# Third down piece made in the next expert's first tile, and the down-weight load placed behind the turned product

## The reference, cut to what matters

```
logits = x @ gate_weight.T ; topk_w, topk_idx = top_k(softmax(logits), 8) ; topk_w /= sum(topk_w)
for every expert e, over the tokens that picked it:
    g = tokens @ w_gate[e]          # 1024 -> 384
    u = tokens @ w_up[e]            # 1024 -> 384
    out = (silu(g) * u) @ w_down[e] # 384 -> 1024
y[token] = sum over its 8 experts of topk_w * out
```

## Time and profile before

| what | value |
| --- | --- |
| median of three runs | 6529.13 us (6527.38 to 6531.33) |
| the profiled execution, its own time | 6549.64 us |
| its span, first to last instruction | 6548.0 us |
| PE busy | 6384.2 us (97%) |
| PE weight loads busy | 5657.9 us (86%) |
| DVE, ACT, POOL busy | 3679.3 (56%), 2889.7 (44%), 2091.6 us (32%) |
| granted TensorE clock, mean over the span | 0.991 |

### The profile page before, as it was taken

How to read it: one execution, slowest core, us unless ns; L and a number is a source line. 1 busy time by engine, 2 the same in 40 slices (tenths; PEclk the granted TensorE clock), 3 DMA queues, 4 the chain that set the end, 5 groups by cost and what they waited for, 6 DMA issues and landing times.

```text
span 6548.0 us, 105789 instructions
## 1 busy us (share of the span) xinstructions
PE 6384.2 (97%) x31912; PEld 5657.9 (86%) x31913; DVE 3679.3 (56%) x4585; ACT 2889.7 (44%) x3319; POOL 2091.6 (32%) x1889
## 2 busy tenths in 40 slices
PE   9999998999999999889999999999999999999998
PEld 7888887887888788779989999999999999999997
DVE  4443434999999899845454455443533444444444
ACT  3222224888888755433343344332422333333333
POOL 1010000000000145644444454444444444444444
PEclk9999999999999999989999999999999999999999
DMA  8754565555555576557676676665755556666666
GB/s 279 244 193 147 148 148 145 130 128 126 126 130 130 144 202 173 134 134 191 164 219 167 175 200 175 170 161 112 194 112 110 139 140 170 147 159 168 164 156 157
DMA packets 844890, 1049.59 MB, mean 160 GB/s; under 512 B 440705, under 2 KB 638081, under 8 KB 844802
## 3 DMA queue, kind: packets, MB, share of 16 engines
q0 software_dynamic: 123984, 368.70, 25.1%
q1 hardware_dynamic: 564432, 382.50, 23.6%
q10 hardware_dynamic: 156386, 297.29, 13.3%
HBM read 725.85 MB, written 322.31 MB: 160 GB/s over the span
## 4 chain that ended last, share of the span: by engine, by line
PE 49%; DMA 2%; issue 2%; DVE 2%; another core or an unknown queue 1%; POOL 1%; ACT 1%; DVEq 1%; ACTq 0%; POOLq 0%; SPq 0%
PE moe_ps_gate L1400 6%; PE moe_ps_gate L1402 5%; PE moe_ps_gate L1401 5%; PE moe_ps_y L1389 5%; PE moe_ps_y L1388 5%; PE moe_ps_up L1401 5%; PE moe_ps_up L1400 5%; PE moe_ps_up L1402 5%; PE moe_ps_y L1387 5%; PE moe_ps_hT L1407 1%; DMA moe_tokens<-h2st,moe_rows 1%; DMA first_raw<-in_w_up 1%; POOL moe_tokens L1342 1%; DVE moe_gu_lo L1508 0%
## 5 line engine op out<-in xcount | busy, mean ns | idle before, releaser
L1342 POOL DMA_INDIRECT moe_tokens<-h2st,moe_rows x1156 | 1228.8, 1063 | 1942.7 <-DVE moe_rows L1518 1674.3
L1400 PE MATMUL moe_ps_gate<-moe_gu_hi,moe_xT_hi 128*128 128x384 f32 x2288 | 794.5, 347 | 61.5 <-DVE moe_xT_lo L1512 43.5
L1401 PE MATMUL moe_ps_gate<-moe_gu_lo,moe_xT_hi 128*128 128x384 f32 x2288 | 769.3, 336 | 0.0
L1400 PE MATMUL moe_ps_up<-moe_gu_hi,moe_xT_hi 128*128 128x384 f32 x2288 | 764.9, 334 | 4.2 <-DVE moe_gu_lo L1508 4.2
L1402 PE MATMUL moe_ps_gate<-moe_gu_hi,moe_xT_lo 128*128 128x384 f32 x2288 | 768.2, 336 | 0.0
L1402 PE MATMUL moe_ps_up<-moe_gu_hi,moe_xT_lo 128*128 128x384 f32 x2288 | 764.3, 334 | 0.0
L1401 PE MATMUL moe_ps_up<-moe_gu_lo,moe_xT_hi 128*128 128x384 f32 x2288 | 764.2, 334 | 0.0
L1531 DVE SCALAR_TENSOR_TENSOR moe_hidden<-moe_hidden,moe_rec_w,moe_ps_up 128x384 f32<-128x384 f32 x286 | 175.3, 613 | 989.1 <-PE moe_ps_up L1402 798.4
L1436 ACT CAST moe_xT_hi<-moe_ps_turned 128x1024 fp32r<-128x1024 f32 x287 | 291.3, 1015 | 908.0 <-PE moe_ps_up L1402 709.0
L1524 DVE STREAM_TRANSPOSE moe_ps_turned<-moe_tokens 128x1024 f32<-128x1024 f32 x288 | 362.5, 1259 | 569.9 <-DMA moe_tokens<-h2st,moe_rows 554.8
L1389 PE MATMUL moe_ps_y<-moe_d_hi,moe_hT_lo 128*128 128x512 f32 x1722 | 676.6, 393 | 0.0
(11 more groups left out here) (205 smaller groups left out, 13426.0 us busy)
## 6 DMA issues: line engine op xcount, KB each, us to landing
first_raw<-in_w_gate ACTq DMA_DIRECT2D x63, 1536.0 KB
first_raw<-in_w_up ACTq DMA_DIRECT2D x63, 1536.0 KB
moe_raw_d<-in_w_down ACTq DMA_DIRECT2D x63, 1536.0 KB
proj_a_raw<-in_ctxT POOLq DMA_DIRECT2D x64, 512.0 KB, 5.7
kst<-proj_o SPq DMA_DIRECT2D x256, 128.0 KB, 2.8
vst<-proj_o SPq DMA_DIRECT2D x64, 512.0 KB, 2.6
qst<-proj_o SPq DMA_DIRECT2D x256, 128.0 KB, 2.2
att_kt<-kst SPq DMA_DIRECT2D x64, 512.0 KB
```

Source lines behind the costliest of these rows:

```text
L1342: nc.gpsimd.indirect_dma_start(out=tokens[:, g * (H // G):(g + 1) * (H // G)], out_offset=None, in_=h2_quarters, in_offset=bass.IndirectOf ...
L1400: nc.tensor.matmul(o[:, 0:I], xT_hi[:, c], gu_hi[:, b, k, c], start=(c == 0), stop=False)
L1401: nc.tensor.matmul(o[:, 0:I], xT_hi[:, c], gu_lo[:, b, k, c], start=False, stop=False)
```

## The change

On DVE, `split` behind an expert's last tile ends one piece earlier, so it makes pieces 4 and 5 only. Piece 6, the third low piece of the down weights, is made in the new expert's own first tile, behind `hidden` and `tokens_low` and ahead of the gate and up pieces for the expert after. The same holds for the very first expert and for the last. ACT still makes the high parts of all seven pieces where it did. On ACT, `load_down` stands behind `turned_high` and no longer between pieces 0 and 1.

```
@@ ACT @@
                 def first_tile(t, e, b, more):
                     tokens_high(t + 1)
-                    split(e, b, 0, 1)
+                    split(e, b, 0, 2)
+                    turned_high(t)
                     load_down(e)
-                    split(e, b, 1, 2)
-                    turned_high(t)
                     split(e, b, 2, 3)
                     output(t - 1)
                     split(e, b, 3, GU)
@@ DVE @@
-                def tile(t, e=None, b=None):
+                def tile(t, e=None, b=None, own=None):
...
                     tokens_low(t + 1)
+                    if own is not None:
+                        split(own, 1 - b, PIECES - 1, PIECES)
                     if e is not None:
                         split(e, b, 0, 3)
                     turn_tokens(t + 2)
...
-                split(0, 0, GU // 2, PIECES)
+                split(0, 0, GU // 2, PIECES - 1)
...
                 def expert(e, b, has_next, has_second):
                     if has_next:
-                        expert_tiles(dve, e, lambda t: tile(t, e + 1, 1 - b), tile)
-                        split(e + 1, 1 - b, GU, PIECES)
+                        expert_tiles(dve, e, lambda t: tile(t, e + 1, 1 - b, e), tile)
+                        split(e + 1, 1 - b, GU, PIECES - 1)
                     else:
-                        expert_tiles(dve, e, tile, tile)
+                        expert_tiles(dve, e, lambda t: tile(t, None, 1 - b, e), tile)
```

## The result

| | kernel before | changed kernel |
| --- | --- | --- |
| median, same session | 6529.45 us (6527.38 to 6536.07, 6 runs) | 6555.22 us (6552.07 to 6560.64, 6 runs) |
| profiled execution, its span | 6549.64, 6548.0 us | 6560.64, 6559.0 us |
| PE busy, share of the span | 6384.2 us, 97% | 6389.3 us, 97% |

The ratio is 1.0039 (95% interval 1.0029 to 1.005). The change makes the kernel 25.8 us slower, clear of the 0.2% that a measurement can tell. The forecast was +9 us, the range up to +39.

The account below looks back on a forecast made before the run. PE, 97% busy, was taken as the bound, with some 50 us lost in the experts' pass. From the profiled 6549.6 us, +12.3 (branch) and -3.0 (load) gave 6558.9; the +9.3 carried to the median: 6538 us, range 6522 to 6568.

Parts of the forecast that it names:

- The likeliest case: Whole kernel: the forecast of 6538 us, given chance 0.50 with its own range of 6530 to 6546 us.
- the slower cases: Outcomes slower than the 0.2% band: forecast's upper part 0.10, unmoved header 0.18, long branch stall 0.08; together 0.36.
- Step 1: DVE, first tiles: without piece 6 ahead, `hidden` and the tokens' low part come 1.14 us earlier where DVE holds them.
- DVE's long header doesn't move: Rival, chance 0.18: in 25 first tiles `hidden` stays put and piece 6 adds some 1.1 us each; 6567 us.
- Steps 2 and 3: PE, first tiles' ends: wait renamed from tokens' low part to piece 6, sum 0.0 us; branch behind it adds 0.32 us.
- step 3: PE's wait now stands on the branch: 0.32 us more, 42 of 56 first tiles later, +12.3 us in sum.
- First ends: PE's loss from first tiles' down product to next tile, against 4.37 us, over 56 tiles: 11.4 us, forecast +12.3.
- The base: Profiled execution lies 20.5 us above the runs' median; the difference of +9.3 us was taken to carry over.
- Step 4: Six one-tile experts: PE waits for the next gate piece, 1.7 us behind piece 6, which hides the branch; 0 us.
- Step 5: DVE's later first-tile work starts at the old time or up to 0.2 us later, covered by over 1 us; 0 us.
- Step 6: `load_down` about 3 us later delays nothing and frees the token gather behind two-tile experts; about -3 us.

Follow-up runs that it names:

- e1: The kernel before run again with no edit, with a new profile: 6533.21 us, ratio 1.0002.
- e7: The changed kernel without PE's wait for all seven pieces, with pieces 5 and 6 both made behind the tokens' low part: 6561.11 us, ratio 1.0046.
- e5: The changed kernel with PE's wait for all seven pieces moved off the branch to the head of each further tile: 6551.64 us, ratio 1.0030.
- e4: The changed kernel with PE's wait for all seven pieces at a first tile's end left out: 6547.31 us, ratio 1.0022.
- e3: The changed kernel with `load_down` back between pieces 0 and 1, so only piece 6 is moved: 6559.46 us, ratio 1.0037.
- e2: The kernel before with only `load_down` moved behind `turned_high`, all pieces at their old places: 6546.6 us, ratio 1.0023.
- e6: The changed kernel without PE's wait for all seven pieces, two thirds of the down load at the old place, one third behind `turned_high`: 6546.6 us, ratio 1.0025.
- e11: The kernel before with `load_down` behind silu at the first tile's end, just ahead of the gate load: 6591.66 us, ratio 1.0057.
- e9: The kernel before with `load_down` behind `output` on ACT, pieces untouched: 6554.76 us, ratio 1.0032.
- e10: The kernel before with `load_down` between the gate and the up load, pieces untouched: 6621.48 us, ratio 1.0134.

## Why the prediction was right and where it was not

The range (6522 to 6568) held the time, and the sign was among the slower cases that I had given 0.36. The likeliest case missed by 17 us. By the prediction's own sign (a tile's average moves by more than 0.05 us) it was wrong: 22.8 us over 285 tiles are 0.08 us against e1; against the profile of before, 12.7 us, they are 0.045.

*Step 1, hidden 1.14 us earlier: in part.* In 20 of the 21 odd-numbered experts behind four or more tiles `hidden` moves from 2.25 (e1) to 0.80 on the scale, 1.45 us; in the 15 even-numbered ones from 2.52 to 1.83 as a rule, 0.69 us, and its "issue" grows from 1.52 to 1.94 us. One odd-numbered expert, DVE with PE's zero, in e1 and in the changed kernel:

```profile
4844.73 0.61 DVE L1531 SCALAR_TENSOR_TENSOR moe_hidden<-moe_hidden,moe_rec_w,moe_ps_up 128x384 f32<-128x384 f32 x1 [1.27 <-issue]
```
```profile
4842.46 0.39 PE L1387 MATMUL moe_ps_y<-moe_d_hi,moe_hT_hi 128*128 128x512 f32 x1
```
```profile
4853.64 0.61 DVE L1530 SCALAR_TENSOR_TENSOR moe_hidden<-moe_hidden,moe_rec_w,moe_ps_up 128x384 f32<-128x384 f32 x1 [0.98 <-PE moe_ps_up L1402]
```
```profile
4852.80 0.39 PE L1387 MATMUL moe_ps_y<-moe_d_hi,moe_hT_hi 128*128 128x512 f32 x1
```

So the rival "DVE's long header doesn't move" holds by half in every second expert, and these are the late ones: 13 of the 15 have a second tile, and in 12 of these piece 6 makes PE start at 5.16 to 5.39. What binds this header was not found; in e7, with one piece ahead of it, it costs nothing.

*Steps 2 and 3, the wait renamed, with the branch on top: right.* PE waits for the down piece 15 times (three of them behind one-tile experts). The distance is 0.48 us, where I had taken 0.32; e5 gives 0.24 of it to the branch. First ends go from 3.9 us (e1) to 16.5 us: +12.6, and the sum of step 3 said +12.3. That agreement is partly luck. I had the waits of the old profile (11.4 us) as the base and 0.32 us on 42 of 56 tiles; in truth the base is 3.9 us, and 15 tiles pay 0.79 us or more each. The sentence "Where DVE is the bound, five pieces of work in another order end at the same time" was right; but in the typical execution DVE is just not the bound there (tokens' low part at 4.27 in even experts, 0.05 us under the limit), so the third piece, which was behind nobody before, is now the last to come.

*The base: the failed step.* "The profiled execution is 20.5 us above the median of the runs; the difference of +9.3 us carries over." It does not. Ten of these 20 us lie in the pass that is changed (3698.3 against 3688.2 us), at the very places that the argument was about (first ends 11.4 against 3.9 us, ends behind one-tile experts 13.9 against 10.1). The "remote" waits ahead of them are absent in e1 and in the changed kernel. Against e1 the profiled difference is 6559.0 - 6535.3 = 23.7 us. Against the old profile it is 11.0 us, close to the forecast's 9.3, but by other terms: first ends +5.1 us and not +12.3, the down product's waits +7.6 us and not 0.

*Step 4, one-tile experts at 0 us: wrong, and by the prediction's own mechanism.* "The branch is hidden under this piece." It is not. Behind a one-tile expert PE passes the branch and the next expert's header, and in the changed kernel it starts 2.2 to 2.7 us behind the end of piece 6 (0.48 at the other first ends). The first gate piece is ready 1.7 to 1.9 us behind piece 6, so PE is late for it by a part: its distance from the gate piece is 0.49 to 0.88 us, six times, where in e1, e4 and e5 it is 0.05 or 0.06 us, six times each. The ends behind these six experts are 4.1 us longer than in e1, and e5 has 3.9 of it back, more than it gains at all first ends together (2.5 us). One such place in the changed kernel, then in e5, which has the wait off the branch. The first of the three pieces in the `x3` row takes 1.75 us and ends at 5784.16 and at 5777.94:

```profile
5781.28 1.21 DVE L1507 TENSOR_TENSOR moe_d_lo<-moe_raw_d,moe_d_hi 128x1024 fp32r<-128x1024 f32 x1
5782.41 5.09 DVE L1507 TENSOR_TENSOR moe_gu_lo<-first_raw,moe_gu_hi 128x1536 fp32r<-128x1536 f32 x3
5784.98 0.44 PE L1400 MATMUL moe_ps_gate<-moe_gu_hi,moe_xT_hi 128*128 128x384 f32 x1 [1.55 <-DVE moe_gu_lo L1507]
```
```profile
5776.19 5.09 DVE L1507 TENSOR_TENSOR moe_gu_lo<-first_raw,moe_gu_hi 128x1536 fp32r<-128x1536 f32 x3
5778.00 0.45 PE L1402 MATMUL moe_ps_gate<-moe_gu_hi,moe_xT_hi 128*128 128x384 f32 x1 [0.80 <-DVE moe_gu_lo L1507]
```

*Step 5, DVE's later work at 0 us: wrong in e7, open in the changed kernel.* PE's waits for the turned product's low part, 7.9 us in e1, are 11.7 us after the change and 29.2 in e7. In e7 they stand behind experts with two tiles too. In the changed kernel four of the five, 11.2 us, stand behind one-tile experts, where DVE itself waits for up weights (next).

*Step 6, the load later, -3 us: the wait goes as predicted, the gain does not come.* The turning of tokens behind two-tile experts waits no more, as predicted: 0 us in 11 places against 17.3 us (16.0 in e1). But the changed kernel is no faster than e3, which has the piece moved and the load in its old place. The answer to the earlier trace rows in the changed kernel, DVE, ACT and POOL:

```profile
4045.40 1.25 DVE L1523 STREAM_TRANSPOSE moe_ps_turned<-moe_tokens 128x1024 f32<-128x1024 f32 x1
```
```profile
4041.75 0.40 ACTq L1453 DMA_DIRECT2D moe_raw_d<-in_w_down  x1
```
```profile
4040.22 1.07 POOL L1342 DMA_INDIRECT moe_tokens<-h2st,moe_rows  x1 [0.30 <-issue]
```

Here the load is behind the last gather issue, and the load alone (e2) shows the other side. Behind a one-tile expert the gate, up and down weights queue back to back, and ACT waits there for the up weights, 3.37 us in e1 and 4.11 us after the change. The down load was issued at 5783.77 after the change and at 5765.70 in e1, 1.21 us ahead and 4.56 us ahead of the next expert's first matmul (5784.98 and 5770.26). Then (ACT in e1, ACT after, PE after):

```profile
5788.71 1.48 ACT L1430 CAST moe_gu_hi<-first_raw 128x1536 fp32r<-128x1536 f32 x1 [3.37 <-DMA first_raw<-in_w_up]
```
```profile
5805.75 1.48 ACT L1430 CAST moe_gu_hi<-first_raw 128x1536 fp32r<-128x1536 f32 x1 [4.11 <-DMA first_raw<-in_w_up]
```
```profile
5810.80 0.79 PE L1387 MATMUL moe_ps_y<-moe_d_hi,moe_hT_hi 128*128 128x512 f32 x1 [3.06 <-DVE moe_hT_lo L1540]
...
5814.32 0.39 PE L1389 MATMUL moe_ps_y<-moe_d_hi,moe_hT_lo 128*128 128x512 f32 x1
```

The up weights come 18.45 us behind that first matmul in e1 and 20.77 us after the change; PE's wait there is 0.56 us in e1 and 3.06 us now. It is tempting to blame the later down load. The record speaks against it: in e2 this load stands as late as in the changed kernel (4.95 us behind the down product's start in both), and the up weights still come 18.39 us behind that first matmul:

```profile
5793.65 1.48 ACT L1430 CAST moe_gu_hi<-first_raw 128x1536 fp32r<-128x1536 f32 x1 [3.38 <-DMA first_raw<-in_w_up]
```

With the piece moved they come at 20.80 us in e3, 20.03 in e4 and 21.22 in e5, and at 20.68 in the profiled run of e6, with two thirds of the load early. PE's waits for the turned product's low part behind the six one-tile experts say the same: 7.4 us in e1 and 4.6 in e2, but 8.7 in e3, 11.2 in the changed kernel, 12.5 in e5 and 15.5 in e4. The single places scatter (behind the first one-tile expert e1 has 22.01 us), and how moving the piece delays the up weights stays open.

*The account.* Against e1, the changed kernel's 22.8 us: first ends +12.6 (forecast +12.3); ends behind one-tile experts +4.1 (10.1 to 14.2; forecast 0); down product +3.8 (7.9 to 11.7; forecast 0); up pieces -2.8 (5.3 to 2.5); loop exits and ends of other tiles +1.2; the load's -3 of the forecast is not found. That is 18.9. The rest, 3.9 us, is of the size of what TensorE's clock costs (last section).

## What to carry to other kernels

A piece of work that is moved off one chain is put in front of another: before moving it, ask of each later item on that engine (here the turning of tokens and the low part of the turned product) how much room it has, and of each wait whose meaning changes without an edit what it now waits for and what stands behind it, on both sides of a branch. Take the base of a sum from more than one profile, and if the profiled execution is out of the range of the timed ones, find the waits that make it so before a difference is carried over. A load is early or late only against the other transfers: place it by what is issued next to it, and try the experts with the least work, where loads queue back to back.

## What the runs showed of the hardware

*TensorE's clock behind a wait.* In the experts' pass of the changed kernel there are seven stretches of 3.4 us at half clock (1.2 GHz), each beginning within 1.5 us of the end of an idle time of PE of 1.80 to 3.53 us. In the profile of before one of 2.11 us is followed by none. Stretches of the changed kernel, with busy times and counts, then granted clock, DMA share and GB/s:

```profile
3328.70:3332.30 3.60, 0.13 (x1) 0.00 (x0) 3.48 (x5) 2.76 (x4) 0.00 (x0) 1.00 1.00 376
3332.40:3335.80 3.40, 3.40 (x9) 2.68 (x10) 2.10 (x3) 1.01 (x1) 2.76 (x2) 0.55 0.78 220
3336.00:3339.40 3.40, 3.40 (x19) 2.92 (x18) 1.01 (x1) 0.70 (x2) 2.49 (x4) 0.97 1.02 357
```

PE was idle for 3.53 us ahead of 3332.36. At 5810.80, above, the same happens behind 3.06 us: eight matmuls take until 5814.32, 3.52 us, where eight take 1.95 us in e1 at the same tile. So this wait cost 1.6 us more than its own length. Within the pass the half clock covers 10.2 us in e1 (three stretches) and 23.9 us after the change (seven). At 1.6 us each the four more are an estimate of some 6 us, somewhat more than the rest of the account.

*One kernel, two levels.* The medians of the kernel before were 6529 to 6533 us in five sets of runs and 6552.36 us (9 runs) in the sixth, on a chip that served no other experiment. The profiled time of before, 6549.64 us, lies within the sixth set (6545.23 to 6555.07) and above all runs of the others (at most 6539.05). There e11's silus show the "remote" wait (14 of them), as in the profile of before and in no other trace. What it waits for the trace doesn't say.

*A DMA issue overtakes.* In e9 a load that stands behind a copy went out 0.79 us before the copy started (3425.35 and 3426.14); so its place in the program is not its place in time.

*Three loads at once.* In e10, behind a one-tile expert, the gate weights landed 7.2 us behind their issue, the down weights 14.8 us, and all traffic (some 5.8 MB, of which 4.72 MB are the three loads) was done 19.4 us behind the first issue, 297 GB/s; a stretch of 2 us in the time of the down load ran at 416 GB/s. A load that stands last in such a group lands with the end of the whole queue.
